# A routed layer's tail: when the two halves of the expert results are loaded, and in which order they are summed and normalised

## The reference, cut to what matters

```
x = x + layernorm(attn(layernorm(x)) @ mixer_w.T + mixer_b)     # x: 2 x 2048 tokens x 128
xt = layernorm(x)                                               # 4096 tokens, H = 128
logits = xt @ gate_w.T                                          # E = 8 experts
idx = top_k(logits + beta, 2)
c[token, idx] = sigmoid(logits[token, idx])
eo_e = (silu(xt @ gate_e) * (xt @ up_e)) @ down_e               # M = 256
combined = sum_e c[:, e] * eo_e
shared = (silu(xt @ sg) * (xt @ su)) @ sd
x = x + layernorm(combined + shared)
```

## Time and profile before

| | us |
|---|---|
| median of 3 runs | 297.49 |
| lowest and highest | 294.58, 304.08 |
| the profiled execution | 299.4 |
| its span, first to last instruction | 297.4 |

### The profile page before, as it was taken

One profiled execution on the slowest core, in us unless ns is written; L12 is line 12 of the kernel. 1 busy time (PEld: TensorE's weight loads), 2 busy tenths in 40 slices (PEclk: granted clock), 3 DMA queues, 4 the chain that ended last, 5 costly groups with the idle time before them and its releaser, 6 DMA issues.

```text
span 297.4 us, 5858 instructions
## 1 busy us (share of the span) xinstructions
PE 242.7 (82%) x1268; PEld 166.7 (56%) x1270; DVE 171.2 (58%) x796; ACT 136.5 (46%) x502; POOL 161.5 (54%) x210
## 2 busy tenths in 40 slices
PE   8999739495988377885989879898988998989990
PEld 3876625252533133433878658776776866869550
DVE  4679767565677528483565455545544545540396
ACT  3874833543455114352445444445434535540571
POOL 7946666363757742745255455554655555654350
PEclk9999977688999655999699999999999999999997
DMA  6991011110111110443022232222213122102983
GB/s 159 264 334 35 22 54 36 36 44 30 47 35 49 56 36 9 118 111 93 18 73 75 72 81 61 74 74 73 73 57 94 47 78 73 57 29 45 389 318 114
DMA packets 28315, 26.34 MB, mean 89 GB/s; under 512 B 7014, under 2 KB 22259, under 8 KB 28288
## 3 DMA queue, kind: packets, MB, share of 16 engines
q1 hardware_dynamic: 22448, 15.38, 18.9%
q0 software_dynamic: 4320, 8.53, 8.1%
q10 hardware_dynamic: 1520, 2.10, 1.9%
HBM read 14.77 MB, written 11.68 MB: 89 GB/s over the span
## 4 chain that ended last, share of the span: by engine, by line
PE 57%; DVE 19%; issue 7%; another core or an unknown queue 7%; ACT 4%; DMA 3%; POOL 1%; POOLq 0%; ACTq 0%; DVEq 0%
PE bank L1386 11%; PE bank L1362 8%; PE bank L1278 6%; PE bank L1378 5%; PE bank L1360 5%; PE bank L1361 4%; PE bank L1148 3%; PE bank L1341 3%; PE bank L1252 2%; DMA xnT<-expert_results 2%; PE bank L1164 2%; DVE x L823 2%; DVE work L1084 2%; DVE X L1135 1%
## 5 line engine op out<-in xcount | busy, mean ns | idle before, releaser
L544 POOL DMA_INDIRECT expert_results<-eo,rowt x71 | 69.8, 983 | 62.3 <-DVE eo L1092 41.9
L526 POOL DMA_INDIRECT expert_rows<-src,slot x64 | 62.7, 980 | 46.0 <-DVE slot L922 28.2
L721 ACT ACTIVATE work<-bank 128x256 f32<-128x256 f32 x71 | 27.5, 387 | 58.9 <-PE bank L1362 52.4
L1386 PE MATMUL bank<-down,work 128*128 x284 | 46.9, 289 | 7.3 <-ACT work L728 3.7
L1084 DVE TENSOR_TENSOR work<-work,bank 128x256 f32<-128x256 f32 x71 | 29.8, 419 | 38.1 <-ACT work L721 19.0
L1386 PEld LDWEIGHTS bank<-down,work 128*128 128x128 f32 x284 | 38.0, 195 | 11.3 <-issue 9.6
L1278 PE MATMUL bank<-xT,gu_f 128*128 128x512 f32 x64 | 39.1, 738 | 0.8 <-DVE xnT L929 0.4
L1092 DVE TENSOR_SCALAR eo<-bank,rowt 128x128 f32<-128x128 f32 x71 | 24.6, 347 | 25.7 <-PE bank L1386 20.3
L1378 PE MATMUL bank<-ident,work 128*128 128x128 f32 x142 | 28.5, 283 | 8.3 <-DVE work L1084 8.0
L1360 PE MATMUL bank<-gu_hi,rh 128*128 x71 | 35.2, 495 | 0.0
L728 ACT ACTIVATE work<-bank 128x256 f32<-128x256 f32 x71 | 27.6, 389 | 9.4 <-PE bank L1378 6.2
(11 more groups left out here) (192 smaller groups left out, 439.7 us busy)
## 6 DMA issues: line engine op xcount, KB each, us to landing
rowt<-expert_rows SPq DMA_DIRECT2D x71, 66.0 KB
X<-n_L_attn_in_sequence_bwc SPq DMA_DIRECT2D x8, 256.0 KB, 3.8
X<-expert_results SPq DMA_DIRECT2D x8, 256.0 KB, 6.8
xnT<-expert_results ACTq DMA_DIRECT2D x8, 256.0 KB, 7.5
out<-X SPq DMA_DIRECT2D x7, 256.0 KB, 2.8
expert_results<-eo,rowt POOLq DMA_INDIRECT x71
gu_f<-in_L_ffn_gate_proj_w SPq DMA_DIRECT2D x1, 1024.0 KB, 7.0
gu_f<-in_L_ffn_up_proj_w SPq DMA_DIRECT2D x1, 1024.0 KB, 9.6
```

Source lines behind the costliest of these rows:

```text
L526: nc.gpsimd.indirect_dma_start(rows_d, bass.IndirectOffsetOnAxis(ap=slot[i % SRC][:, n // TOPK, n % TOPK:n % TOPK + 1], axis=0), src[i % S ...
L544: nc.gpsimd.indirect_dma_start(res_d, bass.IndirectOffsetOnAxis(ap=rowt[v][:, P:P + 1].bitcast(U32), axis=0), eo[v][:], None, bounds_check ...
L721: nc.scalar.activation(sgate[v % 2], gu_ps[v % 2][:, 0:M], ACT.Silu).then_inc(slot_silu, 1)
L1386: last = mm(y_ps[u], hidT[u][:, a, :], down[:, e, a, :], start=a == 0, stop=a == MC - 1)
```

## The change

- Results: where a token's first choice is the last expert, its two result rows change halves (the added term is T = 4096 for the first and -T for the second, times the flag `chosen[:, :, 0, E - 1]`). So no result of the last expert lies in the first half. One copy of 8 numbers per step becomes two operations on 4 each.
- Three table parts (12 to 14) count, for each v, the stores of slots that lie before the last expert's.
- SyncE waits for these counts alone, and issues the 8 loads of the first half; then it waits for all stores, and issues the even pieces of the second half, ScalarE's queue the odd ones.
- VectorE adds the halves of units 1, 2 and 3, before any other work of the tail. TensorE adds both halves in all other units.
- The shared rows of steps 0 to 5 are turned by transposes. TensorE's order is new: shared rows of step 6 behind the last sum of unit 0, those of step 7 with their units.
- `ROOT` is 4. The Newton steps are split: two instructions ahead of a unit's last multiply-and-add, one behind it, two after.

```diff
+                for k, by in enumerate((T, -T)):
+                    nc.vector.scalar_tensor_tensor(
+                        out=src[u][:, k, :, P:P + 1].rearrange("p i a -> p (i a)").bitcast(I32),
+                        in0=chosen[:, :, 0, E - 1], scalar=float(by),
+                        in1=ids[:, k, i // QS, i % QS * G:(i % QS + 1) * G], op0=ALU.mult, op1=ALU.add)
...
+                elif n == 12:
+                    nc.vector.tensor_scalar(ahead[:], iota_r[:], ends[1][:, E - 2:E - 1], 16.0, ALU.is_lt,
+                                            ALU.mult).then_inc(tab_c, 1)
...
+            sp.wait_ge(first_table, 1)
+            counts = [sp.value_load(ahead_i[0:1, v:v + 1], min_val=16, max_val=16 * uses(v)) for v in range(UNROLL)]
+            for v in range(UNROLL):
+                sp.wait_ge(res_out[v], counts[v])
+                sp.sem_inc(waits_apart, 1)
+            for s in range(STEPS):
+                sp.dma_start(tiles(first_y, s), res_v[:, 0, s * G:(s + 1) * G, :]).then_inc(y0_in[s], 16)
             for v in range(UNROLL):
                 sp.wait_ge(res_out[v], 16 * uses(v))
-            for s in range(STEPS):
-                sp.dma_start(tiles(first_y, s), res_v[:, 0, s * G:(s + 1) * G, :]).then_inc(y_in[s], 16)
+            for s in range(0, STEPS, 2):
+                sp.dma_start(tiles(second_y, s), res_v[:, 1, s * G:(s + 1) * G, :]).then_inc(y1_in[s], 16)
...
-                        mm(part, yshT[:, s, i * P:(i + 1) * P], ident[:], start=i == at, stop=False,
+                        mm(part, yshT[:, s, i * P:(i + 1) * P], ident[:], is_transpose=True, start=i == at, stop=False,
                            skip_group_check=True)
...
+            for n in range(DIRECT):
                 add_shared(n)
+            add_first(0)
+            for n in range(4, DIRECT):
+                add_first(n)
+            add_last(0)
+            add_shared(DIRECT)
+            for n in range(1, DIRECT):
+                add_last(n)
+                if n == 3:
+                    add_first(DIRECT)
+            add_last(DIRECT)
```

More of the change, by code:

```diff
@@ L324, in build_sandwich @@
         res_out = [sem(f"res_out{v}") for v in range(UNROLL)]
-        y_in = [sem(f"y_in{n}") for n in range(STEPS)]
+        y0_in = [sem(f"y0_in{n}") for n in range(STEPS)]
+        y1_in = [sem(f"y1_in{n}") for n in range(STEPS)]
         z0_done = sem("z0_done")
@@ L737, in _ @@
                 act.wait_ge(res_out[v], 16 * uses(v))
-            for s in range(STEPS):
-                act.dma_start(tiles(second_y, s), res_v[:, 1, s * G:(s + 1) * G, :]).then_inc(y_in[s], 16)
+            for s in range(1, STEPS, 2):
+                act.dma_start(tiles(second_y, s), res_v[:, 1, s * G:(s + 1) * G, :]).then_inc(y1_in[s], 16)
             act.wait_ge(route_consts, 1)
@@ L1101, in _ @@
             slots(routed, 2, dve)
[L1104 to L1128, removed]
-                        dve.wait_ge(newton_c, at_c + 3)
-                        nc.vector.scalar_tensor_tensor(
-                            out=rstd[u][:, 1, 0:count], in0=guess2[u][:, 0:count], scalar=1.5, in1=guess[u][:, 0:count],
-                            op0=ALU.add, op1=ALU.mult).then_inc(newton_c, 1)
-                        dve.wait_ge(newton_c, at_c + 4)
-                    for i in range(count):
-                        last = nc.vector.scalar_tensor_tensor(
-                            out=tile(first_y, s, at + i), in0=z_ps[m][:, i * P:(i + 1) * P],
-                            scalar=rstd[u][:, 1, i:i + 1], in1=tile(x1, s, at + i), op0=ALU.mult, op1=ALU.add)
-                    last.then_inc(sum_done, 1)
@@ new lines, in newton @@
+            def newton(m, part):
+                if not ROOT <= m < UNITS:
+                    return
+                u, count, at_c = m % 2, units[m][2], (m - ROOT) * 4
+                half, y, t = (x[:, 0:count] for x in (vpe[u][:, 1, :], guess[u], guess2[u]))
+                if part == 0:
+                    dve.wait_ge(sumsq4_done, m + 1)
+                    nc.vector.tensor_scalar(half, sumsq[u][:, 0:count], -0.5 / P, -0.5 * EPS, ALU.mult, ALU.add)
+                    dve.wait_ge(root_done, m - ROOT + 1)
+                    nc.vector.reciprocal(y, root[u][:, 0:count]).then_inc(newton_c, 1)
+                    return
+                dve.wait_ge(newton_c, at_c + part)
+                if part == 1:
+                    nc.vector.tensor_tensor(t, y, y, ALU.mult).then_inc(newton_c, 1)
+                elif part == 2:
+                    nc.vector.tensor_tensor(t, t, half, ALU.mult).then_inc(newton_c, 1)
+                else:
+                    nc.vector.scalar_tensor_tensor(out=rstd[u][:, 1, 0:count], in0=t, scalar=1.5, in1=y, op0=ALU.add,
+                                                   op1=ALU.mult).then_inc(newton_c, 1)
@@ new lines, in _ @@
+            for n in BY_DVE:
+                dve.wait_ge(y0_in[n], 16)
+                dve.wait_ge(y1_in[n], 16)
+                nc.vector.tensor_tensor(tiles(first_y, n), tiles(first_y, n), tiles(second_y, n),
+                                        ALU.add).then_inc(z0_done, 1)
+            for m, (s, at, count) in enumerate(units):
+                u = m % 2
+                if m < ROOT:
+                    dve.wait_ge(ln4_c, m * 2 + 2)
+                else:
+                    dve.wait_ge(newton_c, (m - ROOT) * 4 + 4)
+                for i in range(count):
+                    last = nc.vector.scalar_tensor_tensor(
+                        out=tile(first_y, s, at + i), in0=z_ps[m][:, i * P:(i + 1) * P],
+                        scalar=rstd[u][:, 1, i:i + 1], in1=tile(x1, s, at + i), op0=ALU.mult, op1=ALU.add)
+                    if i == count - 1:
+                        last.then_inc(sum_done, 1)
+                    if i >= count - 2:
+                        newton(m + 1, i - count + 2)
+                newton(m + 1, 2)
+                newton(m + 1, 3)
```

44 lines of the change are left out of this document (30 added, 14 removed).

## The result

| | before | changed |
|---|---|---|
| runs | 294.58, 304.08, 297.49, 301.04 | 304.81, 307.51, 305.55, 306.81 |
| median | 299.26 | 306.18 |
| profiled execution, span | 299.4, 297.4 | 304.81, 303.0 |

The ratio is 1.034, with an interval of 1.022 to 1.046: the changed kernel is slower. The forecast was 297.3, with a time within 2% of before as by far the likeliest, and its range ended at 301.0. (Ratios leave out runs over 1.5% above the fastest of their kernel, so they do not always follow the medians of all runs.)

What follows compares the result with a forecast made beforehand. The prediction took the tail as bound first by the results' transfer, then by four engines in a row with VectorE last. Tail -0.45 plus routing +0.25 gave -0.2 us, so 297.3 from 297.49, range 293.8 to 301.0.

Steps and rivals of the forecast that it cites:

- tail: From the last store's start to the end of VectorE's last multiply-and-add; forecast to change by -0.45 us.
- the first sentence on the second half: Second half's first load: issued at 272.86 as before, with the last store landing 2.09 us after its start.
- its rival of 277.9: Second half's first piece, sharing engines with first-half loads, usable at 277.9 instead of 276.6; +1.3 us, chance 0.22.
- a last store that lands later than 2.1 us after its start: Listed sign, at the last store before the second half's loads, that the forecast is wrong; no size given.
- The rival by SyncE's queue: Second half's first piece stands behind first-half loads in SyncE's queue; +1.3 us on the forecast, 298.6, chance 0.22.
- B: From issue of the second half's first load to the last multiply-and-add's end; forecast 21.8 us, before 22.3.
- the Newton units: VectorE's units from unit 4 on, split so a wait runs beside other work; forecast 1.77 us apart, before 1.91.
- unit 1's squares: ScalarE's start on unit 1 in the tail; forecast near 280.6, after unit 0's second-half product at 276.6.
- the clock: TensorE idles from 274.8 and its clock falls to half in the sums; 3.5 us or more, 300.8, chance 0.06.
- 267.7: Issue of the first half's first load, once slot 66's store lands 2.09 us after its start at 265.47.
- SyncE's reading of the counts: SyncE's wait on counts ahead of the first half's loads; claimed to hold nothing up.
- 0.25: Routing: two operations for one copy, 8 times, on the chain in three steps; +0.25 us, bounds 0 and 1.4.

Runs made afterwards that it cites:

- e3: Kernel before with swapped halves, table parts 12 to 14 and the early loads of the first half, tail's work as before; 253.73 us, ratio 1.029 to before.
- e10: Changed kernel whose eight early loads read the input x instead of the results; 254.96 us in one run, with before at 245.75.
- e16: Changed kernel again, unaltered; 297.56 us, ratio 0.997 to before.
- e17: Changed kernel once more, unaltered, with more runs; 303.75 us, ratio 1.027 to before.
- e2: Kernel before with the swapped halves and table parts 12 to 14, and nothing that uses them; 249.41 us, ratio 1.016 to before.
- e1: Changed kernel with all loads of results behind all stores, first half on SyncE's queue, second on ScalarE's; 255.96 us, ratio 1.042 to before.
- e6: Changed kernel again, unaltered; 300.0 us, with before at 299.67.
- e7: Kernel before with the swap of halves alone, no tables or early loads; 301.77 us, with before at 299.67.
- e8: Kernel before with the three table parts alone, no swap; 298.64 us, with before at 299.67.
- e15: Kernel before with transposes for shared rows, ROOT 4, split Newton steps, and both halves' loads waiting only for filled slots' stores; 292.11 us, ratio 0.984 to before.
- e18: Second run of before with transposes, ROOT 4, split Newton steps and loads waiting only for filled slots' stores; 297.28 us, ratio 1.004 to before.
- e4: Changed kernel with only three first-half pieces early, five behind all stores, whole second half on ScalarE's queue; 255.25 us, ratio 1.031 to before.
- e14: Kernel before with transposes for the shared rows, ROOT 4 and split Newton steps; 294.87 us, ratio 0.989 to before.
- e11: Kernel before with both halves' loads waiting only for stores of slots that hold rows, no swap, nothing early; 246.30 us, ratio 0.998 to before.

## Why the prediction was wrong

**The step that failed** is the first sentence on the second half: "It is issued at 272.86 as before, since the last store waits for GpSimd and not for this." The store starts when GpSimd comes to it, and that held; but the loads wait for its landing, and that was taken as 2.09 us, whatever else the engines carry. It was 6.64, and 4.8 to 6.3 in the four others with 8 early pieces whose chain runs over it (e3, e10, e16, e17). The prediction worked out how two streams share the engines for the second half's first piece (its rival of 277.9) and did not ask it of the stores that the second half waits for. It named the sign only at its end, as "a last store that lands later than 2.1 us after its start". So the sum lacked a term of +4.5 us (6.78 - 2.24). With it the sum gives 301.8. Of the other 4.4 us to the 306.2 measured, 1.8 are the last store's later start, and 1.8 the median of before, which was 299.26 over four runs where the sum started from 297.49. The rival by SyncE's queue gave 298.6 by another way and is not what happened: when the second half was issued, the first was through, and 3.6 us later TensorE had its piece (282.84), about as before (276.65 - 272.86 = 3.8).

**What held.** B was 21.5 us, where 21.8 was forecast and 22.3 stood before; the Newton units were 1.76 us apart; unit 1's squares followed 3.98 us behind unit 0's second-half product (282.84 to 286.82), where 276.6 to 280.6 was forecast. That is a gain of 0.8 us, a sixth of the loss. It held in this trace alone: over the four traces of the changed kernel B is 22.7 on average, against 22.4 in those of before, as in the other three the clock fell in the sums.

**Smaller misses.** The first half was issued at 270.48 and not at 267.7: in seven traces it goes out 3.5 to 4.6 us behind the start of slot 66's store, not 2.2. This is the store's own landing: in e2 and e1, where nothing is loaded early, its count is full only 3.8 and 3.5 us after its start, fifteen of the sixteen increments having come by 2.1. The prediction took the 2.09 us of slot 70's empty store for a store that has 4 rows. SyncE's reading of the counts held nothing up, as was said: it ended at 261.8, ahead of that store. And the clock: the prediction gave its fall 0.06, as TensorE idled from 274.8. It fell in each of the four traces of the changed kernel. In the first it fell before the arrival, at no cost; in e16, e6 and e17 it fell in the sums, and B is 2.9, 0.7 and 1.2 us longer than in the first (for e16 and e17 the chains put this on TensorE's products, 2.7 and 1.6 us; for e6 it is argued).

**The size.** Over four traces the changed kernel's tail is 29.1 on average, over four of before 24.6: 4.5 us, or 1.5% of 299. The medians' differences on the four chips of this kind with both kernels are 6.9, 0.3, 1.7 and 4.3 us, on average 3.3, and the ratios 1.034, 0.997 (e16) and 1.027 (e17), with none for e6. So the first measurement's 6.9 is at the high end. Whether the stages ahead of the tail pay too is open. The last store's start lay 1.84 us later in the first trace, but 1.5 and 4.4 earlier in e6 and e16 than in the traces of before on their chips, which speaks against it. For it speak the ratios of 1.034 and 1.027, above the tail's 1.5%, and e2: swap and tables measured +1.6% on a chip of 246 us, 3.7 us, where the forecast had 0.25, while its profile has before's tail, and e1, with the same edits, comes to its last store 3.4 us sooner. Where these 3.7 us are, and whether they exist on the other chips (e7 +2.1, e8 -1.0, both within scatter), stays open.

**A version without the early stream.** e15 and e18 load both halves once the filled slots' stores have landed. Their tails are 22.0 and 22.3, 2.2 to 2.7 us shorter than the 24.5 to 24.6 of before on chips of the same kind. The ratios to before are 0.984 and 1.004, so that it beats the kernel before is shown for the tail, and not for the whole. Against the changed kernel, the intervals are apart on one chip (0.998 to 1.009 against 1.019 to 1.035) and overlap on the other.

## What to carry to other kernels

When a transfer is brought forward, ask first what small transfers are still to land beside it, and who waits for those: their landing time is a price, not a constant. A wait on a count of stores ends when the last one lands, and 2 MB of loads that start 2 us before it cost more here (4.5 us) than they saved. Where a store carries nothing that the loads need, as the two empty slots' here, leave it out of the wait. And a saving behind cover on TensorE can cost: here an engine that idled before the work that counts did that work in part at half its clock.

## What the runs showed of the hardware

- The indirect store of an empty slot lands 2.1 us after its start with no loads beside it (e1, e2), 3.7 with 3 pieces of 256 KB begun 0.8 us ahead (e4), 4.8 to 6.6 with 8 begun 0.8 to 2.0 us ahead. The delay lies ahead of its own packets.
- A store of 128 rows lands 2.25 us after its start (e2, slot 64), one with 4 rows 3.5 to 3.8 (slot 66 in e1, e2 and e11, no early loads).
- TensorE's clock fell to 0.50 of 2.4 GHz in tails in which it idled ahead of the sums (busy for 0.31 of 3 us in e14), and the 16 passes that take 1.78 us at full clock took 3.41 (e16).
- A transpose of 128 x 128 in one pass takes 0.11 us, so 24 took 2.8 us in e15, where the 48 passes of the product with the identity took 5.60.
- The same kernel takes 296 to 300 us on some chips and 246 on others, with the same tail (24.5 to 24.9).
